# Eight bf16 identity products into an unread PSUM bank at the end of each softmax step and each hyperbolic chunk

## The reference

```python
# layer 0: softmax aggregation, per feature, over the edges of a target node
m = relu(feats[src] + edge_h) + EPS
ex = exp(m - segment_max(m, dst)[dst])
h = segment_sum(m * ex / segment_sum(ex, dst)[dst], dst)
# layer 1: mean over the edges
agg = segment_sum(x[src], dst) / max(deg, 1)
# layer 2: hyperbolic attention, over the edges sorted by their source node (row)
e = -2 / sqrt(c) * arctanh(clip(sqrt(c) * |mobius(-hh[row], hh[col])|))
att = segment_sum(exp(e) / denom[row] * log_h[col], row)
# layer 3: relational attention, softmax over the edges of a target node
s = leaky_relu(el[rel, src] + er[rel, dst])
h = segment_sum(feat_all[rel, src] * softmax(s, by=dst), dst)
```

## Time and profile before

| | us |
|---|---|
| median of 3 runs | 12268.7 (12235.75 to 12348.68) |
| the profiled execution | 12218.17 |
| its span, first to last instruction | 12216.4 |
| edge stage of layer 0, first to last gather | 233 to 2725 |
| edge stage of layer 1 | 3047 to 5531 |
| edge stage of layer 2 | 6138 to 9268 |
| edge stage of layer 3 | 9564 to 11998 |

### The profile page before, as it was taken

How to read it: one execution, slowest core, us unless ns; L and a number is a source line. 1 busy time by engine, 2 the same in 40 slices (tenths; PEclk the granted TensorE clock), 3 DMA queues, 4 the chain that set the end, 5 groups by cost and what they waited for, 6 DMA issues and landing times. The chain is left out here.

```text
span 12216.4 us, 120473 instructions
## 1 busy us (share of the span) xinstructions
PE 6560.5 (54%) x28159; PEld 5236.5 (43%) x28159; DVE 6951.0 (57%) x14143; ACT 4184.0 (34%) x8456; POOL 7235.6 (59%) x7482
## 2 busy tenths in 40 slices
PE   0655555553155555552356666666665555555552
PEld 0333333332145555551356666666664333333331
DVE  3556555667355555541645555555555477777775
ACT  0222222222055555551134444444444322222221
POOL 5666666664656666666155555555554666666665
PEclk9666666665577777775555555555556666666665
DMA  4333333332422222222033333333334444444442
GB/s 89 108 110 109 111 110 107 111 109 47 134 54 56 56 55 56 55 56 27 12 85 78 78 78 79 79 77 79 77 78 114 117 114 114 113 114 115 114 114 78
DMA packets 1318230, 1059.32 MB, mean 87 GB/s; under 512 B 815857, under 2 KB 1034376, under 8 KB 1316531
## 3 DMA queue, kind: packets, MB, share of 16 engines
q0 software_dynamic: 238720, 318.69, 13.9%
q1 hardware_dynamic: 681698, 373.56, 12.0%
q10 hardware_dynamic: 397397, 362.35, 9.1%
HBM read 580.99 MB, written 472.73 MB: 86 GB/s over the span
## 5 line engine op out<-in xcount | busy, mean ns | idle before, releaser
L1172 POOL DMA_INDIRECT h_rows_d<-table,h_idx_d x1840 | 1750.6, 951 | 1389.1 <-PE h_ps_sum L1192 812.6
L648 POOL DMA_INDIRECT rows<-table,idx_all x1664 | 1643.0, 987 | 870.8 <-issue 476.0
L955 POOL DMA_INDIRECT m_rows<-table,idx_all x1664 | 1575.0, 947 | 911.0 <-issue 453.2
L648 POOL DMA_INDIRECT rows<-table3s,idx_all x1664 | 1574.4, 946 | 872.5 <-issue 476.0
L985 PE MATMUL m_ps_sort<-m_hot_high,m_hot_low 128*128 128x224 f32 x3328 | 1056.9, 497 | 973.6 <-issue 818.2
L985 PEld LDWEIGHTS m_ps_sort<-m_hot_high,m_hot_low 128*128 128x128 f32 x3328 | 920.2, 283 | 1081.5 <-issue 941.0
L795 PE MATMUL ps_out<-ident,sums 128*128 128x128 f32 x3328 | 776.7, 398 | 965.6 <-issue 690.5
L1192 PE MATMUL h_ps_sum<-h_rows_d,h_hot 128*128 128x65 f32 x3680 | 832.0, 417 | 635.6 <-DVE h_rows_d L1329 352.1
L795 PEld LDWEIGHTS ps_out<-ident,sums 128*128 128x128 f32 x3328 | 629.9, 221 | 1131.5 <-issue 1075.6
L1192 PEld LDWEIGHTS h_ps_sum<-h_rows_d,h_hot 128*128 128x128 f32 x3680 | 795.4, 328 | 719.9 <-issue 719.9
L1210 PE MATMUL h_ps_src<-h_near,h_hot_t 128*128 128x65 f32 x3680 | 838.2, 419 | 462.1 <-DMA h_near<-table 252.8
(11 more groups left out here) (425 smaller groups left out, 14233.0 us busy)
## 6 DMA issues: line engine op xcount, KB each, us to landing
scan<-out_e ACTq DMA_DIRECT2D x832, 256.0 KB
h_near<-table SPq DMA_DIRECT2D x1840, 32.5 KB
run_g<-h_run ACTq DMA_DIRECT2D x230, 260.0 KB
part_b<-part SPq DMA_DIRECT2D x832, 64.0 KB
max_b<-top ACTq DMA_DIRECT2D x416, 128.0 KB
scan<-m_out_e SPq DMA_DIRECT2D x416, 128.0 KB
attr<-in_edge_attr SPq DMA_DIRECT2D x415, 128.0 KB
h_rows_d<-table,h_idx_d POOLq DMA_INDIRECT x1840
```

Source lines behind the costliest of these rows:

```text
L648: pool.indirect_dma_start(out=rows[:, b, k, h * GW:(h + 1) * GW], out_offset=None, in_=table3s.rearrange("n (q f) -> (n q) f", f=HEADS) if ...
L955: pool.indirect_dma_start(out=rows[:, b, k, h * D:(h + 1) * D], out_offset=None, in_=table1, in_offset=bass.IndirectOffsetOnAxis(ap=idx_al ...
L1172: pool.indirect_dma_start(out=rows_d[:, b, k, :], out_offset=None, in_=table2, in_offset=bass.IndirectOffsetOnAxis(ap=idx_d[:, c * BT + k: ...
```

## The change

After `to_rows` of each softmax step and after `turn_hot` of each hyperbolic chunk TensorE runs eight products of a bf16 identity with a bf16 identity that is repeated four times (128 x 512), in a function `keep_going`. They wait for nothing and signal nothing. They write to a PSUM bank that nobody reads: in layer 0 and in the hyperbolic stage a bank of their own, in layer 3 the upper 64 partitions of the bank whose lower 64 hold `ps_v`. In the softmax stages the stationary operand is half the identity (64 columns). All sizes, buffers, semaphores and other engines' lists stay as they were.

```diff
@@ softmax_edges @@
                 if rel:
                     ps_mult = psum("ps_mult", [P, 2, W])
-                    ps_v = psum("ps_v", [HALVES * REL_HEADS, W])
+                    ps_v_p = psum("ps_v", [P, W])
+                    ps_v = ps_v_p[0:HALVES * REL_HEADS, :]
+                    ps_spare = ps_v_p[HALVES * REL_HEADS:P, :]
+                else:
+                    ps_spare = psum("ps_spare", [P, W])[0:P // 2, :]
...
+                        def keep_going(c, b, r):
+                            for j in range(8):
+                                nc.tensor.matmul(ps_spare, ident_b[:, 0:P // 2], ident_b[:, None, :].broadcast_to([P, TILES, P]),
+                                                 start=True, stop=True)
+
                         if rel:
-                            written_out(STEPS, (0, v_columns), (1, score_columns), (3, to_rows))
+                            written_out(STEPS, (0, v_columns), (1, score_columns), (3, to_rows), (3, keep_going))
                         else:
-                            written_out(STEPS, (0, to_columns), (1, count), (2, to_rows))
+                            written_out(STEPS, (0, to_columns), (1, count), (2, to_rows), (2, keep_going))
@@ hyperbolic_edges @@
+                ps_spare = psum("ps_spare", [P, W])
...
+                        def keep_going(c, b, r):
+                            for j in range(8):
+                                nc.tensor.matmul(ps_spare[:, :], ident_b[:, :], ident_b[:, None, :].broadcast_to([P, W // P, P]),
+                                                 start=True, stop=True)
+
-                        steps(pe, CHB, (3, add_up), (1, expand), (0, turn_hot))
+                        steps(pe, CHB, (3, add_up), (1, expand), (0, turn_hot), (0, keep_going))
```

## The result

The kernel with the eight products took 12472.91 us (median of three, 12469.24 to 12480.25) against 12268.7 before: a ratio of 1.0168 (95% interval 1.0136 to 1.0199). It is 1.7% slower where a gain of 1.0% was forecast. The profiled execution took 12480.25 us, 262 us more in its span than the one of before.

The account below looks back on a forecast made before the run. POOL's gathers with their round trip, not TensorE's rate, were taken to set three of four stages. 0 + 50 - 160 = -110 us from 12268.7 gave 12159, put at 12150 us with the `expand` part; range 11750 to 12700.

Parts of the forecast that it names:

- What bounds the kernel: Edge stages: POOL's gathers (10.0 us per eight) and their round trip, not TensorE's rate, set three of four stages.
- Price of eight products: TensorE: the eight added products cost about 3.2 us at the low clock level and 1.9 at the high one.
- Layer 0: Layer 0, 208 steps: POOL's burst and return hide the products, so 0 us.
- +94: Layer 0 without POOL's cover: a delay of 0.9 us per pair over 104 pairs, 94 us.
- rival 1: Products, mainly ahead of `v_columns` in layer 3, cost more than they bring: up to +499, 12770 us; chance 0.31.
- Layer 3: Layer 3, 208 steps: products delay DVE 1.05 to 2.35 us per pair, mostly swallowed by POOL's return: +50 us.
- the bound of +244: Layer 3 with all the delay exposed: 104 pairs at 2.35 us, +244 us.
- Hyperbolic: Hyperbolic stage, 230 chunks: the higher clock shortens `add_up` and POOL's wait for it, -160 us; ends -365 and +161.
- half of it: Half of the possible loss of +499 us over layer 0, layer 3 and the hyperbolic stage: 12520 us.
- rival 2: Hyperbolic stage: POOL paces it too, gains and costs cancel, nothing comes of the change: 12270 us; chance 0.20.
- Rival 3: All stages: the higher clock frees them toward POOL's 10.0 us, 10660 at best, 11730 us taken; chance 0.07.
- what would show it: Signs in the later trace; for slower: layer 3 stretch over 2500 us and DVE's scan waiting for `v_columns` every step.

Follow-up runs that it names:

- the repetition: The whole change, all eight products in all their stages, measured again against the kernel before: 12254.66 us against 12008.72, ratio 1.0251.
- only_l3: The eight products in layer 3 alone, none in layer 0 and the hyperbolic stage, against the kernel before: 10058.22 us against 10063.14, ratio 0.9996.

## Why the prediction was wrong

- **What bounds the kernel: right.** POOL's bursts and their return set the stages; halving a burst took 4.4 us off a step. "This wait belongs to the bursts and not to the clock" holds: at 0.70 in place of 0.51 the signal of `turn_hot` comes 1.91 us behind the burst, before 1.84 (median of the long pauses), and behind bursts half as long hardly any result is late. The prediction did not see that the lateness differs from chip to chip.
- **Price of eight products: right in the main.** Eight span 1.91 to 3.62 us in layer 3, 2.77 in the median; the bounds were 1.9 and 3.2. The upper one was short: eight spacings of 0.427 us alone are 3.4, and the last record is longer than its spacing. Inside the eight of the timeline above the products start 0.427 us apart at first (10511.504, 10511.933, 10512.359, 10512.786) and 0.216 at the end (10513.109, 10513.326, 10513.542, 10513.758): the clock rises while the eight run. Of the 2912 spacings in layers 0 and 3, 1252 lie at 0.42 to 0.43 us and 1296 at 0.21 to 0.22. The trace agrees with the Trainium skill (TensorE: Matmul & The Clock Gate, Back-to-back issue gap), whose 512 / 1.2 and 512 / 2.4 + 2.5 ns are 0.427 and 0.216 us.
- **Layer 0: right.** 0 forecast, +11 us measured (at a clock of 0.75 for 0.65). One of its numbers is a slip: 1540.59 lies 2.39 us behind 1538.2 and not 2.3, so its +94 should be +84, and the 499 of rival 1 489.
- **Layer 3: the step that failed.** "in the second POOL's return covers it" and "so most is swallowed: I take +50". The shift itself was sized well (1.05 to 2.35 us a step; 1.41 measured). But nothing swallowed it. The scan waits in every step and not in the first of each pair, and pauses of over 1 us stand behind 156 bursts in place of 102. Of these 49 in place of one are over 5 us, because the result of `v_columns` is held over the burst and scan, `own_v`, `weighted` and `ps_mult` run behind it, 4.09 us. Measured +200, +160 to +219 and +138 to +198 us in three comparisons. That this is near the bound of +244 is chance: the bound was a shift of 2.35 us in each pair, and not long pauses in a quarter of the steps. The experiment with the products behind `v_columns` shows a third to a half of it to be the place; with the products behind it 24 long pauses are left (one in the unchanged layer 3), and why they are still there is open.
- **Hyperbolic: the other step that failed.** 365 us were "the most that a faster TensorE can return", and I took 180. `add_up` did get 1.68 us shorter in half or more of the long waits, but the term left out that `add_up` waits for a message whose own input, the result of `expand`, is one of TensorE's late results. Pauses that hang on it got 1.2 us shorter, and 96 in place of 57 (in the repetition 1.3 us shorter, and 69 in place of 48). And `expand` hardly saw the higher clock. Measured +34, +5 and +26 us in place of -160.
- **The rivals.** Rival 1 was the case in its mechanism and its place (ahead of `v_columns`). That "half of it", 12520 us, stands 47 us from the measured time is luck: it was half of all three terms, and measured were +11, +200 and +34 against bounds of 94, 244 and 161. It had 0.31. It would have deserved more, for the earlier trace rows already set a slack of 0.85 us against a price of 1.9 at least: a certain delay, against a swallowing that no row showed. The time of rival 2 is what prompt chips show. Rival 3 is refuted: layer 0 with 0.75 takes no less than with 0.65. A higher clock did not make the kernel faster in any of the runs, so the penalty that the Trainium skill (TensorE: Matmul & The Clock Gate, HAM oscillation) counts for throttled time is no time of this kernel.
- Of what would show it, the layer 3 stretch over 2500 us and the scan waiting in every step came as rival 1 said.

## What to carry to other kernels

A higher granted clock is worth something only where TensorE's rate is on the path; ask for each faster product what it waits for, and whether that input moves. Work put in "idle" time of an in-order engine delays what stands behind it: hold its length against the slack of the next result, and if it is longer, count a loss until a row shows that it is swallowed. Behind the result that others wait for it cost less here, but not nothing (128 for 198 us). Where a wait has two lengths, count how often each comes: a mean or a median hides that short ones became long. And read a small change of this kind stage by stage, on more than one chip.

## What the runs showed of the hardware

- The same kernel takes 10063 to 10065 us on two chips and 11973 to 12269 in the four other measurements. On the former a result of TensorE reaches its reader 0.09 us after its record (8801.96 to 8802.05), on the latter some take 9.8 us (10524.95 to 10534.71). The semaphore events say the same: in layer 3 of `only_l3` all 208 signals of `v_columns` stand within 0.02 us of their product's end, in the kernel before 102 of the 151 that the trace has are over 1 us late, 7.6 us in the median. Whether the gathers hold the results or only the semaphores, or something that both share, no run here tells.
- The late results come about 1.8 us behind a burst of 8 gathers (hyperbolic stage) and 3.4 us behind one of 16 (layer 0 before). With bursts of 4 on a late chip they are late no longer (2 of 207 signals over 1 us).
- fp32 products right behind the bf16 eight ran in 305 ns for 417 on average, those of `expand`, behind a longer idle time, in 396 for 419.
